# A two-layer decoder on one core: a mask moved from matmuls into the instruction that takes the row maximum, with a new order of pieces

## The reference, cut to what matters

```python
x = x + L0_attn(ln(x))                 # causal attention, quantised weights
x = x + L0_xattn(ln(x), ctx)           # WKV recurrence over time
x = x + L0_ffn(ln(x))                  # gated, ternary weights
x = x + L1_attn(ln(x))                 # 32 heads, rotary positions
x = x + L1_xattn(ctx, ln(x))           # cross attention, below
x = x + L1_ffn(ln(x))                  # base matrix plus routed low-rank experts
```

```python
kcat = concat([k_of_ctx, k_of_x], axis=2)           # 2 x 128 keys
ssm_mask = (delta >= 0) & (delta < 64)              # delta = query - key
att_mask = (delta >= 0) & (delta < 32)
scores = einsum('bhqd,bhkd->bhqk', q, kcat) / sqrt(8) + bias
scores = where(concat([ssm_mask, att_mask]), scores, -inf)
o = einsum('bhqk,bhkd->bhqd', softmax(scores), vcat)
```

## Time and profile before

| what | value |
|---|---|
| median of 3 runs | 688.61 us |
| lowest and highest | 686.31 and 689.04 us |
| span of the profiled execution | 691.1 us |
| PE, DVE, ACT, POOL busy | 613.2, 543.6, 481.4, 392.3 us |
| mean granted clock of PE | 0.949 of full speed |

### The profile page before, as it was taken

One profiled execution on the slowest core, in us unless ns is written; L12 is line 12 of the kernel. 1 busy time (PEld: TensorE's weight loads), 2 busy tenths in 40 slices (PEclk: granted clock), 3 DMA queues, 4 the chain that ended last, 5 costly groups with the idle time before them and its releaser, 6 DMA issues.

```text
span 691.1 us, 20216 instructions
## 1 busy us (share of the span) xinstructions
PE 613.2 (89%) x7368; PEld 372.6 (54%) x7368; DVE 543.6 (79%) x1357; ACT 481.4 (70%) x1185; POOL 392.3 (57%) x745
## 2 busy tenths in 40 slices
PE   6699999856788789999999988789999999999984
PEld 6466666534566568544444344345555556555542
DVE  5889999899899996889998867567777777777521
ACT  4599998996878646577787773467676667666650
POOL 5343786897899958856665312334545544545321
PEclk9799999998899989999999999899999999999995
DMA  8899645111110002444545524353343444433000
GB/s 296 205 220 170 93 94 107 57 58 39 39 39 32 24 11 54 64 78 89 79 79 86 95 58 81 60 89 68 76 82 73 68 80 88 79 76 59 20 9 15
DMA packets 163603, 55.11 MB, mean 80 GB/s; under 512 B 148976, under 2 KB 161456, under 8 KB 163376
## 3 DMA queue, kind: packets, MB, share of 16 engines
q1 hardware_dynamic: 161456, 53.68, 38.1%
q0 software_dynamic: 2048, 0.14, 0.2%
HBM read 16.82 MB, written 5.24 MB: 32 GB/s over the span
## 4 chain that ended last, share of the span: by engine, by line
PE 57%; DVE 18%; issue 7%; POOL 6%; DMA 6%; ACT 4%; SPq 1%; DVEq 0%; ACTq 0%; POOLq 0%
PE bank L1333 4%; PE bank L1266 4%; PE bank L1002 3%; PE bank L1280 3%; PE bank L1678 3%; DMA l1x_qT<-l1x_neg_maxT 3%; DVE mix_num_den L1542 2%; PE bank L1355 2%; PE bank L1305 2%; DMA l1a_kT<-k_stack 2%; PE bank L1287 2%; PE bank L1863 2%; PE bank L976 2%; PE bank L1689 2%; PE bank L1022 2%
## 5 line engine op out<-in xcount | busy, mean ns | idle before, releaser
L1181 DVE TENSOR_REDUCE l1x_neg_max<-bank 128x2 f16<-128x448 f32 (+1 forms) x192 | 116.0, 640 | 46.3 <-PE bank L1287 46.1
L1235 ACT ACTIVATE l1x_probs<-bank 128x512 f32<-128x512 f32 x192 | 104.2, 596 | 57.4 <-PE bank L1309 33.0
L889 DVE TENSOR_REDUCE l1a_neg_max<-bank 128x4 f16<-128x512 f32 x128 | 82.2, 685 | 12.9 <-PE bank L976 11.9
L936 ACT ACTIVATE l1a_probs<-bank 128x512 f32<-128x512 f32 x128 | 69.5, 595 | 21.3 <-PE bank L990 21.3
L1137 POOL DMA_DIRECT2D l1x_qT<-l1x_neg_maxT x64 | 37.5, 592 | 51.7 <-ACT l1x_neg_maxT L1231 51.7
L1678 PE MATMUL bank<-mix_xT_parts,w_ternary 128*128 128x256 f16 x384 | 53.1, 287 | 7.7 <-DVE mix_hidden L1560 7.5
L1678 PEld LDWEIGHTS bank<-mix_xT_parts,w_ternary 128*128 128x128 f16 x384 | 38.5, 103 | 19.8 <-DVE mix_hidden L1560 11.2
L1754 POOL TENSOR_TENSOR moe_logits<-moe_low_rank_logits,router_bias 128x6 f32<-128x6 f32 x16 | 3.3, 206 | 77.4 <-ACT moe_low_rank_logits L1831 77.4
L573 DVE TENSOR_REDUCE l_neg_max<-bank 128x4 f16<-128x512 f32 x64 | 41.5, 674 | 5.7 <-PE bank L698 5.0
L1492 POOL TENSOR_TENSOR mix_hidden_parts<-mix_hidden,mix_hidden_parts 128x256 f16<-128x256 f32 x48 | 38.0, 799 | 8.5 <-ACT mix_hidden_parts L1623 8.1
L642 ACT ACTIVATE l_probs<-bank 128x512 f32<-128x512 f32 x64 | 35.2, 608 | 3.5 <-PE bank L721 1.8
(11 more groups left out here) (271 smaller groups left out, 1814.5 us busy)
## 6 DMA issues: line engine op xcount, KB each, us to landing
ctx_projected<-mix_ctx_projected SPq DMA_DIRECT2D x16, 192.0 KB, 2.0
l1x_ctx_projected<-ctx_projected SPq DMA_DIRECT2D x16, 160.0 KB, 2.4
mix_ctx_in<-ctx_in SPq DMA_DIRECT2D x16, 128.0 KB, 2.1
out_dram<-moe_out SPq DMA_DIRECT2D x16, 128.0 KB, 2.1
x_residual<-x_in SPq DMA_DIRECT2D x1, 1536.0 KB, 10.0
w_f<-w_in SPq DMA_DIRECT2D x2, 704.0 KB, 10.3
w_attn_f<-w_l_in SPq DMA_DIRECT2D x4, 256.0 KB, 3.9
q_stack<-q_begin_in SPq DMA_DIRECT2D x1, 1024.0 KB, 6.2
```

What stands on the lines that cost most here:

```text
L889: dve.tensor_reduce(mm[:, 16 * j + 4 * s:16 * j + 4 * s + 4], b_s[c % 3][:].rearrange("p (r k) -> p r k", k=P), AX.X, ALU.max, negate=True ...
L936: act.activation(prob[:, c, :], b_st[c % 2][:], ACT.Exp).then_inc(s_exp, 1)
L1181: dve.tensor_reduce(mm[:, first:first + count], scores, AX.X, ALU.max, negate=True).then_inc(s_max, 1)
L1235: act.activation(prob[:, c, :], b_st[c % 2][:], ACT.Exp).then_inc(s_exp, 1)
```

## The change

1. In `l1x`, pieces S.2 to S.5 on PE no longer add the mask; their key matmuls start the bank's sum. DVE's pieces S.4 to S.11 (two for each) have, in place of one reduction over 2 x 224 columns, two `tensor_tensor_reduce` over 224: each adds the f32 window to the scores, writes the negated sum back into the bank and the minimum of it as the negated row maximum. S.0 and S.1 stay as they are.
2. `window_end` and the two casts that fill it leave POOL (`FITTED` 9 to 7).
3. POOL's rstd pieces (F1c in `l1a` and `l1x`, LNc in `moe`) wait also until the normalised block of two turns back is written.
4. `PHASES`, `PACE` and `STEPS` have new numbers throughout. Merged, they give: on SP all 24 steps of `begin`, with all 17 late loads, before the first G of `l0`; inside the steady part of `l0`, `l1a` and `l1x` single pieces past one or two neighbours; in `mix` more of them.

```diff
 PHASES = {
     ("l0", "sp"): phases("""
-        G@5.030"""),
+        G@11.448"""),
...
     ("l1x", "pe"): phases("""
-        F5@0.040 F7@0.253 S.0@1.543 S.1@1.690 S.2@1.823 S.3@2.029 S.4@2.113 S.5@2.396 M@2.506 ST.0@2.830 ST.1@2.999
-        ST.2@3.150 ST.3@3.432 ST.4@3.653 PV.0@3.684 ST.5@3.743 PV.1@3.843 T1@4.103 T4@4.394 T5@4.435"""),
+        F5@0.106 F7@0.279 S.0@1.674 S.1@1.780 S.2@1.912 S.3@1.999 S.4@2.151 S.5@2.282 M@2.663 ST.0@2.896 ST.1@2.996
+        ST.2@3.155 ST.3@3.344 ST.4@3.682 PV.0@3.708 ST.5@3.727 PV.1@3.950 T1@4.106 T4@4.197 T5@4.383"""),
...
 STEPS = {
-    ("begin", "sp"): (-116.643, -89.445, -85.349, -81.253, -77.158, -73.062, -69.071, -71.307, -68.508, -66.442, -64.376, -62.310, -60.244, -58.179, -56.113, -52.720, -48.222, -43.723, -39.225, -34.726, -30.228, -25.729, -18.805, -10.970,),
+    ("begin", "sp"): (-192.707, -1.897, -285.131, -95.210, -99.384, 90.074, -464.937, -165.269, 126.492, 59.954, -560.279, -310.799, -44.499, -14.445, 153.342, -153.678, 58.620, -215.690, -204.880, -15.656, 82.921, -159.631, 149.992, -176.217,),
...
-    ("l0", "sp"): (-102.007,),
+    ("l0", "sp"): (212.133,),
...
-    for x in range(2):
-        yield next(at)
-        pool.tensor_copy(net.xq1[:, 224 * x:224 * x + 224],
-                         net.xwin[:, 1].rearrange("p e k -> p (e k)")[:, 32:256]).then_inc(net.s_fit, 1)
...
             if piece == "F1c":
                 pool.wait_ge(s_f1, b * 3 + 3)
+                wait(pool, s_xn, b - 1)
                 pool.tensor_tensor(rstd[:, bp, :], ve[:, bp, :], net.mhalf[:], ALU.pow).then_inc(s_rstd, 1)
...
                 if c < 4:
-                    first, count = 16 * j + 4 * (c // 2), 4
-                    scores = bank[:].rearrange("p (r k) -> p r k", k=P)
+                    first = 16 * j + 4 * (c // 2)
+                    ins = dve.tensor_reduce(mm[:, first:first + 4], bank[:].rearrange("p (r k) -> p r k", k=P), AX.X, ALU.max,
+                                            negate=True)
                 else:
-                    first, count = 16 * j + 8 + 2 * (c // 2 - 2), 2
-                    scores = bank[:, 0:448].rearrange("p (r k) -> p r k", k=224)
-                dve.tensor_reduce(mm[:, first:first + count], scores, AX.X, ALU.max, negate=True).then_inc(s_max, 1)
+                    first = 16 * j + 8 + 2 * (c // 2 - 2)
+                    for x in range(2):
+                        ins = dve.tensor_tensor_reduce(bank[:, 224 * x:224 * x + 224], bank[:, 224 * x:224 * x + 224], windows[1][:, 32:256], -1.0, 3e38,
+                                                       ALU.add, ALU.min, mm[:, first + x:first + x + 1])
+                ins.then_inc(s_max, 1)
...
-                width, mask = (512, net.xq0) if z == 0 else (448, net.xq1)
...
-                for j, u, rows, ps in tiles:
-                    pe.matmul(ps[:, 0:width], net.identb[rows, rows], mask[rows, :], start=True, stop=False,
-                              skip_group_check=True)
+                if z == 0:
+                    for j, u, rows, ps in tiles:
+                        pe.matmul(ps, net.identb[rows, rows], net.xq0[rows, :], start=True, stop=False, skip_group_check=True)
...
                         ins = pe.matmul(ps[:, n * x:n * x + n], qt[rows, b % 3, 4 * s + 2 * r2 + u, 64 * z:64 * z + 64], keys,
-                                        start=False, stop=True, skip_group_check=True)
+                                        start=z == 1, stop=True, skip_group_check=True)
```

More of the change, by code:

```diff
@@ L160 @@
     ("moe", "pe"): phases("""
-        TR@4.868 DOWN@5.063 LORA@5.482 UP@5.773"""),
+        TR@4.989 DOWN@5.104 LORA@5.466 UP@5.815"""),
 }
 PACE = {
-    "l0": (-91.729, 19.87, (4.716, 6.971, 8.492, 11.987), 11.788),
-    "mix": (52.728, 7.79, (11.429, 15.313, 7.496, 17.994), 10.483),
-    "l1a": (155.651, 7.256, (10.436, 19.603, 9.301, 1.957), 11.021),
-    "l1x": (339.773, 12.172, (17.067, 4.886, 5.859, 27.864), 28.378),
-    "moe": (340.826, 6.331, (16.814, 4.859, 5.87, 27.849), 28.341),
+    "l0": (-92.744, 64.448, (7.743, 0.989, 11.287, 13.438), 10.087),
@@ L169 @@
+    "mix": (53.178, 5.055, (11.386, 8.577, 10.539, 20.803), 11.177),
+    "l1a": (156.726, 10.211, (10.742, 19.425, 1.021, 8.774), 12.691),
+    "l1x": (339.499, 11.341, (17.235, 4.928, 6.028, 27.175), 27.573),
+    "moe": (341.118, 1255.932, (16.828, 4.963, 5.995, 27.483), 26.912),
 }
 STEPS = {
-    ("begin", "act"): (-145.369, -98.637, -174.919, -104.910, -154.067,),
-    ("begin", "dve"): (-171.500, -170.900, -112.030, -87.641, -105.835, -81.102, -76.678, -70.526, -65.155, -78.842, -42.210, -35.435, -6.383,),
@@ L179 @@
-    ("l0", "pool"): (-55.442,),
-    ("l0", "sp"): (-102.007,),
-    ("mix", "act"): (31.719,),
-    ("mix", "dve"): (8.464,),
-    ("mix", "pe"): (37.056,),
-    ("mix", "pool"): (8.325,),
-    ("mix", "sp"): (66.465,),
-    ("l1a", "act"): (137.865,),
-    ("l1a", "dve"): (98.517,),
-    ("l1a", "pe"): (91.053,),
-    ("l1a", "pool"): (107.294,),
-    ("l1a", "sp"): (216.642,),
-    ("l1x", "act"): (327.195,),
-    ("l1x", "dve"): (313.533,),
-    ("l1x", "pe"): (217.711,),
-    ("l1x", "pool"): (333.214,),
@@ new lines @@
+    ("l0", "pool"): (-159.994,),
+    ("l0", "sp"): (212.133,),
+    ("mix", "act"): (25.496,),
+    ("mix", "dve"): (24.593,),
+    ("mix", "pe"): (12.570,),
+    ("mix", "pool"): (9.553,),
+    ("mix", "sp"): (214.213,),
+    ("l1a", "act"): (141.314,),
+    ("l1a", "dve"): (127.648,),
+    ("l1a", "pe"): (10.265,),
+    ("l1a", "pool"): (102.416,),
+    ("l1a", "sp"): (266.865,),
+    ("l1x", "act"): (323.735,),
+    ("l1x", "dve"): (229.554,),
+    ("l1x", "pe"): (261.795,),
+    ("l1x", "pool"): (267.278,),
@@ L202 @@
+    ("l1x", "sp"): (393.302,),
+    ("moe", "act"): (396.737,),
+    ("moe", "dve"): (392.763,),
+    ("moe", "pe"): (237.284,),
+    ("moe", "pool"): (374.977,),
+    ("moe", "sp"): (327.567,),
+    ("windows", "pool"): (-20.912, -13.098, 14.148, -35.097, -28.316, -15.869, 10.610,),
 }
@@ L1137, in pool_program @@
                         pool.dma_start(dst, mt[r0:r0 + 8, :]).then_inc(s_md, 16)
+    windows = [net.xwin[:, z].rearrange("p e k -> p (e k)") for z in range(2)]
     def dve_program(dve):
@@ L1883, in build @@
         net.xwin = sb("windows_f32", [P, 2, 4, 64])
[L1884 removed]
+        net.xq0 = sb("window_begin", [P, 512], BF16)
         net.xkm, net.identr = sb("window_of_keys", [P, 3, P], BF16), sb("ident_repeated", [P, 512], BF16)
```

92 lines of the change are left out of this document (43 added, 49 removed).

## The result

| | before | after |
|---|---|---|
| median | 688.6 us (686.31 to 689.04, 4 runs) | 701.25 us (698.95 to 703.06, 4 runs) |
| span of the profiled execution | 691.1 us | 699.9 us |
| PE, DVE, ACT, POOL busy | 613.2, 543.6, 481.4, 392.3 us | 598.5, 553.4, 477.8, 386.4 us |

The ratio is 1.0181, 95% interval 1.0143 to 1.0219: slower by 12.6 us (9.8 to 15.1). The range of 679 to 702 held the time by 0.8 us; the likeliest case, 690.6 us, did not happen, and the range given for the forecast alone, 684 to 697, did not hold it. The two spans differ by 8.8 us only, because the profiled execution of before lies above its median: the after one took 701.78 us for a span of 699.9, so with the same 1.9 us around it (an estimate) the 691.1 us of before stand for 693.0, some 4.4 above the median.

A forecast was written before the change was run, and what follows sets the result against it. No one engine was taken to bound the whole; PE bounds the steady cross attention, DVE the mixing stage. 691.1 + 7 (start) - 5 (cross attention) + 0 = 693.1 us, less 2.5 for the median: 690.6 us, range 679 to 702.

The forecast's parts named there:

- The late loads ahead of the first G: Start of l0: 17 loads queued ahead delay block 0's transposes to 36.5 us from 25.43, a raw delay of 11 us.
- Given back: together some 4 us: Start: the third weight sum ahead of the wait, block 1's ready transposes and load-free later transposes recover some 4 us.
- start term: Start of l0: raw delay of 11 us less some 4 recovered, so +7 us, between +3 and +12.
- Other order edits 0 and +-4: Reordered pieces in l0, l1a, l1x and the mixing stage add no work: 0 us, give or take 4.
- The mask edit on PE: Cross attention: four mask matmuls fewer take 4 x 0.19 = 0.76 us a block from PE, at most 9.8 us.
- PE's block becomes 13.96: Cross attention: PE's time per steady block falls from 14.72 to 13.96 us.
- Half given back: Cross attention: with PE waiting for DVE's maximum before reusing a bank, the stage gains 5 us, not 9.8.
- The mask edit on DVE: Cross attention: two new instructions per reduction cost +0.28 us a pair, making DVE's block 13.5 us instead of 11.28.
- low end: Cross attention, DVE: priced like a plain addition, the new pair costs only +0.08 us over the one reduction.
- rival 2: Cross attention: the new instruction is dear and DVE becomes the bound; 700 us at +0.46 a pair; chance 0.20.
- Rival 1: Start: the late loads don't hold the first transposes; 683.6 us; chance 0.27.
- Rival 3: Cross attention's fill and mixing stage: the new order gains more than the start costs; set at 680 us; chance 0.13.

The follow-up runs named there:

- before_loads_first: The kernel before with one table number changed, so that SP issues all 17 late loads before the first transposes: 700.81 us, ratio 1.0170.
- after_loads_between: The kernel after with SP's loads and first transposes back in the old order, all else as after: 690.24 us, ratio 1.0034 to before.
- mask_only: The kernel before with the mask edit alone (points 1 and 2 of the change), in the old order of pieces: 684.91 us, ratio 0.9950.
- order_only: The kernel before with all of after's tables, the old mask and without POOL's three waits: 703.08 us, ratio 1.0207.

## Why the prediction was right or wrong

**The late loads ahead of the first G: right, and undersized.** The queue was full from 25 us on, as the rows above show, and its rate fell from 380 GB/s (30 to 34 us) to 85 (34 to 36 us), at about the 34.4 us that was forecast from the bytes and 378 GB/s. But the first scores came 3.8 us after that, not 2: at 38.17, not 36.5. Raw delay 12.7 us, not 11. before_loads_first and after_loads_between show the place of the loads as the cause of 10 to 12 us from both sides.

**"Given back: together some 4 us": wrong.** This is the step that failed most clearly. In before_loads_first the first scores start 12.4 us late and the time is 11.7 us longer, 9.5 at least: 2.9 us at most came back. Its `l0` runs from first to last maximum in 103.8 us against 104.9, and the third sum, priced at 1.75 us, was worth 1.1 in the trace and nothing measurable in the time; both differences are within the spread of traces of one order. A start term of +11 to +12 in place of +7 gives 694.6 to 695.6.

**"Other order edits 0 and +-4": too low, by how much is open.** 5.8 us (3.8 to 7.8) by after_loads_between against mask_only, 2.5 (-0.5 to 5.5) by order_only against before_loads_first. Two parts are seen in the trace and were not tested by a run of their own. At the start DVE takes `l0`'s pieces and the attention weights in another order: G of block 0 is issued at 23.07 us in after_loads_between, at 19.98 in before, and its maxima start 2.7 us later than in mask_only even with the loads out of the way. A late start was kept almost whole in before_loads_first, so this could be half of the 5.8 (an estimate). And the fillers of PE went behind the first scores; in after they took 3.76 us there, and `l0` took 108.3 us, 4.5 more than in before_loads_first, which starts as late. In after_loads_between, however, with fillers of 3.29 us in the same place, `l0` took 105.0, near the 104.5 of mask_only, so the fillers' price without the late start is hidden or made up for. In the cross attention the new order costs 0.2 us a block (14.54 against 14.33), where DVE has six of the new instructions in a row behind T1; with the old mask it costs nothing there (blocks of 14.72 us in order_only as in before), so it is the two together. POOL's three waits are in after and after_loads_between and in no other kernel, and were not tried by themselves. The rest of the 5.8 us stays open; the profiled execution of after_loads_between was the fastest of that kernel's (span 681.5 for a median of 690.24), so its trace shows too little of it.

**The mask edit on PE: the step right, the way to the floor overlooked.** 0.19 us x 4 left PE as said. But "PE's block becomes 13.96" overlooked two waits of 0.19 us that then appear, for ACT's copy and for DVE's maxima; with both mostly taken away the best blocks reach 14.01. 14.3 us was forecast for the block, 14.54 to 14.56 came in after, 14.33 in the old order. Half given back was the right guess in the old order for a reason that I had only half: PE waits for DVE's maximum, but at M, not for a free bank. For the time, -5 became -3.4 (-4.8 to -2.0) in the old order; in the new one after stands at 1.0181 and order_only at 1.0207, a difference that their intervals don't tell from none.

**The mask edit on DVE: too dear.** +0.16 us a pair, between the low end (+0.08) and the value taken (+0.28); DVE's block is 12.70 us, not 13.5. The read-out is there as the row of line 1182 shows, 256 times, but overlapped to 0.06 us. The rule of the Trainium skill ("VectorE: DVE Perf Modes", section "Two Vector instructions with no wait between them") that such an operation is two instructions agrees with these rows. "Vector Engine (DVE) Microarchitecture Reference" of the Trainium skill, section "7. Points that are easy to get wrong", states its halved throughput for the form `S2S2D2_STT` with two non-bf16 SBUF sources. No run here has two sources in SBUF, nor shows that the new instruction is of that form; 385 and 386 ns for an f32 and a bf16 window beside a bank agree with it and don't test it.

**The sum.** The range was met by luck in part: its upper end, 702, was set by rival 2, whose mechanism did not come, while the forecast itself was 10.7 us too low, 4 to 5 of them by the start term, the rest by the other order and the mask's smaller gain. 693.1 us of span was made against the profiled execution of 691.1 and then lowered by 2.5 for the median. With the measured terms (+11.7 start, +5.8 other order, -3.4 mask) on 688.6 it is 702.7, with +2.5 for the other order 699.4, against 701.25.

**The rivals.** Rival 1 (the loads don't hold the transposes) was excluded by the row at 38.17 us. Rival 2 gave 700 us, close to the result, by another mechanism: it wanted a pair +0.46 and a block above 14.8 with DVE over 95% busy; the block shrank, and DVE is at 87%. The number agrees by chance. A milder form of it is real: DVE doesn't bound the block by its sum but by its sequence ahead of the transposed maxima. Rival 3 was to show in shifts of the later stages: +13.8 and +11.7 us against +12.7 at the start, within the 3 us; the order gave nothing net.

## What to carry to other kernels

An order edit is read first at the queue that it fills: add up the bytes now ahead of the first transfer that something waits for, divide by the rate the trace shows, and don't count on a stage whose PE and DVE are over 90% busy to catch it up (at most 2.9 of 12.4 us here). Work removed from the bounding engine is worth its step only where nothing else was hiding behind it; look, for each removed piece, at what the next instruction's operand was doing meanwhile. And before moving an instruction away from a wait, follow its result through the other queues: making the producer's copy earlier won 0.16 us in the best blocks (14.17 to 14.01), making the consumer later lost 2.7 us of the whole time (687.57 against 684.91).

## What the runs showed of the hardware

- The same addition with a minimum took DVE 425 ns with its 224 f32 results written into a bank and 385 ns with them written to SBUF in bf16, and its read-out 145 against 85; the step fell from 0.35 to 0.31 us. Whether the place or the type of the result does it was not separated.
- The operand's type in SBUF (f32 or bf16) made no difference where the other operand is in a bank: 385 and 386 ns.
- A transpose by DMA issued behind a full queue held SP itself: 9.61 us in one issue, 3.26 in the next, where the later pairs of the same trace take 1.2 to 1.3 each.
- After 14 us without matmuls PE's granted clock was 0.50 (1.2 GHz) until 44 us, and eight fillers took 3.76 us there, 1.95 at 20 us at the higher level. The low clock alone is no mark of the hole: in before it was 0.50 from 30 to 36 us as well, with PE busy 5.66 of 6 us:

```profile
30.00:36.00 6.00, 5.66 (x59) 3.68 (x59) 4.93 (x12) 3.56 (x8) 1.44 (x4) 0.50 1.05 309
```
